# A GNN layer and a mixture of experts on one core: some preparation of the tables done by GpSimd in place of VectorE

## What is computed

```python
def gnn(h, rel, w_ih, w_hh, b_ih, b_hh, src, dst, etype):
    msg = h[src] + rel[etype]
    red = segment_sum(msg, dst, num_segments=6250)
    return gru_cell(red, h, w_ih, w_hh, b_ih, b_hh)

x = x + gnn(layernorm(x), rel, ..., src, dst, edge_type_16)
x = x + experts(layernorm(x))     # top 2 of 8 by x @ Wg + bg; gelu(x @ W1 + b1) @ W2 + b2
```

## Time and profile before

| | |
|---|---|
| median of 3 runs | 1611.08 us (1608.55 to 1616.82) |
| the profiled execution | 1608.13 us |
| its span in the profile | 1606.3 us |
| busy: PE, DVE, ACT, POOL | 83%, 69%, 44%, 64% of the span |
| first gather | 72.29 us |
| last gather | 1195.6 us |

### The profile page before, as it was taken

How to read it: one execution, slowest core, us unless ns; L and a number is a source line. 1 busy time by engine, 2 the same in 40 slices (tenths; PEclk the granted TensorE clock), 3 DMA queues, 4 the chain that set the end, 5 groups by cost and what they waited for, 6 DMA issues and landing times. The chain is left out here.

```text
span 1606.3 us, 37371 instructions
## 1 busy us (share of the span) xinstructions
PE 1333.8 (83%) x12905; PEld 1025.3 (64%) x12905; DVE 1100.4 (69%) x3994; ACT 708.4 (44%) x1538; POOL 1034.2 (64%) x948
## 2 busy tenths in 40 slices
PE   1269999999989999989889998784653899999991
PEld 1235656666656666666667766564653799999991
DVE  7867677577777777778979888953545455555550
ACT  6334444444445554434433332221221676667660
POOL 2177777566777777676777777777773255555552
PEclk9959999999999999999998999686766899999996
DMA  9676544344554455444544544446652455555556
GB/s 304 175 214 197 153 127 114 109 132 133 138 146 137 132 148 143 123 115 142 145 132 146 146 133 112 113 120 211 236 119 60 100 101 94 95 94 96 94 80 179
DMA packets 136158, 220.43 MB, mean 137 GB/s; under 512 B 27761, under 2 KB 101046, under 8 KB 134688
## 3 DMA queue, kind: packets, MB, share of 16 engines
q0 software_dynamic: 63872, 123.12, 31.7%
q1 hardware_dynamic: 72096, 94.84, 19.7%
HBM read 169.05 MB, written 57.76 MB: 141 GB/s over the span
## 5 line engine op out<-in xcount | busy, mean ns | idle before, releaser
L667 POOL DMA_INDIRECT ring<-h_table,idx x728 | 727.2, 999 | 316.2 <-issue 254.8
L780 ACT ACTIVATE amat<-P 128x300 f16<-128x300 f32 (+3 forms) x608 | 230.6, 427 | 398.0 <-PE P L1642 396.2
L1655 PE MATMUL P<-hs,amat 128*126 128x512 f16 (+4 forms) x1323 | 356.9, 399 | 0.0
L721 POOL DMA_INDIRECT out_rows<-yo,xrows x112 | 176.5, 1576 | 162.4 <-DVE yo L1527 114.6
L1140 DVE TENSOR_SCALAR cone<-iota,comb 128x294 f16<-128x294 f16 (+3 forms) x840 | 258.2, 310 | 0.0
L1139 DVE TENSOR_SCALAR lone<-iota,slo 128x128 f16<-128x128 f16 x840 | 223.7, 267 | 15.7 <-PE P L1637 15.2
L1637 PE MATMUL P<-cone,lone 128*128 128x294 f16 (+3 forms) x840 | 164.6, 291 | 52.3 <-ACT amat L780 32.5
L1655 PEld LDWEIGHTS P<-hs,amat 128*126 128x126 f16 (+4 forms) x1323 | 160.7, 137 | 71.9 <-issue 8.2
L1518 DVE SCALAR_TENSOR_TENSOR gl<-gT,scales,gh 128x512 f16<-128x512 f32 x112 | 84.2, 752 | 126.1 <-ACT gh L904 126.1
L1869 PE MATMUL P<-xh,w_all 128*128 128x256 f16 x896 | 157.0, 274 | 0.0
L676 POOL DMA_INDIRECT expert_rows<-xrow,slots x100 | 121.6, 1216 | 54.3 <-issue 26.8
(11 more groups left out here) (240 smaller groups left out, 2666.3 us busy)
## 6 DMA issues: line engine op xcount, KB each, us to landing
raw<-in_L_ffn_W_dram SPq DMA_DIRECT2D x32, 512.0 KB
xrows<-expert_rows SPq DMA_DIRECT2D x56, 257.0 KB, 3.2
ring<-h_table,idx POOLq DMA_INDIRECT x728
w_parts<-parts SPq DMA_DIRECT2D x16, 512.0 KB
w_all<-w_parts SPq DMA_DIRECT2D x8, 1024.0 KB
h_in<-h_table SPq DMA_DIRECT2D x25, 250.0 KB
x<-in_x_dram SPq DMA_DIRECT2D x25, 250.0 KB
out_rows<-x SPq DMA_DIRECT2D x25, 250.0 KB
```

The source lines that it names most:

```text
L667: nc.gpsimd.indirect_dma_start(out=ring[:, r, j, :], out_offset=None, in_=h_dram, in_offset=bass.IndirectOffsetOnAxis(ap=idx[:, slot, g * ...
L721: nc.gpsimd.indirect_dma_start(out=out_dram, out_offset=bass.IndirectOffsetOnAxis(ap=xrows[:, b % XR, j, D:D + 1].bitcast(I32), axis=0), i ...
L780: nc.scalar.activation(amat[:, b % 2, :, s * aw:(s + 1) * aw], P[2 + g % 2][:, 0:HIS * aw].rearrange("p (h w) -> p h w", w=aw), ACT.Copy). ...
L1655: nc.tensor.matmul(both, amat[:, b % 2, hi, 0:used], hs[:, hi, :], start=(hi == 0), stop=False)
```

## The change

Five groups of instructions go from DVE to POOL, in the preamble:
- rest(0), rest(2) and rest(4), with a semaphore `s_rest2`; SP's waits take the one or the other by chunk;
- the splitting of the relation vectors;
- of the source keys the cast of the low bits and the subtraction, which is now float32 on both sides (a cast of the sources first). DVE keeps the mask, ahead of `bases`, and `s_keys` hands it to POOL; `small_weights` waits for POOL's keys.

```diff
+POOL_RESTS = (0, 2, 4)
...
             for c in range(LN_CH + 1):
-                sp.wait_ge(s_rest1, c + 1)
+                if c in POOL_RESTS:
+                    sp.wait_ge(s_rest2, POOL_RESTS.index(c) + 1)
+                else:
+                    sp.wait_ge(s_rest1, c + 1 - sum(n < c for n in POOL_RESTS))
...
 # POOL, behind its two casts, ahead of its waits for s_tr, s_bias and the table
+            def rest(c):
+                pool.wait_ge(s_part1, c + 1)
+                at = hs[:, c * LN_J:c * LN_J + LN_J, :]
+                nc.gpsimd.tensor_tensor(at[:, :, D:PD], xc[:, c % XB, :, :], at[:, :, 0:D], ALU.subtract).then_inc(s_rest2, 1)
+
+            rest(0)
+            rest(2)
+            pool.wait_ge(s_rel, 16)
+            pool_link(nc.gpsimd.tensor_scalar(rel_rest, rel_raw, UP, None, ALU.mult))
+            for part in range(PARTS):
+                pool_link(nc.gpsimd.tensor_copy(rels[:, part, :], rel_rest))
+                if part + 1 < PARTS:
+                    pool_link(nc.gpsimd.tensor_tensor(rel_rest, rel_rest, rels[:, part, :], ALU.subtract))
+            rest(4)
+            pool.wait_ge(s_keys, 1)
+            nc.gpsimd.tensor_copy(slo[:, :], slo_i[:, :])
+            pool_link(nc.gpsimd.tensor_copy(comb[:, :], src_t[:, 0:HEAD * GC]))
+            nc.gpsimd.tensor_tensor(comb[:, :], comb[:, :], slo[:, :], ALU.subtract).then_inc(s_keys, 1)
...
 # DVE, small_weights: the six instructions on the relation vectors go
-                dve.wait_ge(s_rel, 16)
...
+                dve.wait_ge(s_keys, 2)
...
-            rest(0)
             edge_windows()
             rest(1)
             coefficients(3)
             statistics(4)
-            rest(2)
             coefficients(4)
...
             coefficients(6)
-            rest(4)
             rest(5)
             rest(6)
+            dve.wait_ge(s_tr_out, RT)
+            nc.vector.tensor_scalar(slo_i[:, :], src_t[:, 0:HEAD * GC], 127, None, ALU.bitwise_and).then_inc(s_keys, 1)
             bases()
...
 # DVE, head_keys
-                link(nc.vector.tensor_scalar(slo_i[:, :], src_t[:, 0:n], 127, None, ALU.bitwise_and))
-                nc.vector.tensor_copy(slo[:, :], slo_i[:, :])
-                link(nc.vector.tensor_tensor(comb[:, :], src_t[:, 0:n], slo_i[:, :], ALU.subtract))
```

More of the change, by code:

```diff
@@ L451, in gnn_ffn_kernel @@
         names = """
-            s_const s_ones s_pads s_wnat s_weights s_rel s_ln_var s_ln_std s_ln_coef s_ln_h s_part1 s_rest1 s_natf
+            s_const s_ones s_pads s_wnat s_weights s_rel s_ln_var s_ln_std s_ln_coef s_ln_h s_part1 s_rest1 s_rest2 s_keys s_natf
             s_viol s_violb s_natd s_base s_based s_tr s_dst_out s_tr_out s_flag s_bias s_zero s_small s_init
@@ L463, in gnn_ffn_kernel @@
             tx_done xh_ready xl_ready w1_ready l1_done gelu_done g_high g_low l2_done y_out firsts_ready
-            out_written dve_chain late_chain
+            out_written dve_chain late_chain pool_chain
         """.split()
-        (s_const, s_ones, s_pads, s_wnat, s_weights, s_rel, s_ln_var, s_ln_std, s_ln_coef, s_ln_h, s_part1, s_rest1, s_natf,
+        (s_const, s_ones, s_pads, s_wnat, s_weights, s_rel, s_ln_var, s_ln_std, s_ln_coef, s_ln_h, s_part1, s_rest1, s_rest2, s_keys, s_natf,
          s_viol, s_violb, s_natd, s_base, s_based, s_tr, s_dst_out, s_tr_out, s_flag, s_bias, s_zero, s_small, s_init,
@@ L477, in gnn_ffn_kernel @@
          tx_done, xh_ready, xl_ready, w1_ready, l1_done, gelu_done, g_high, g_low, l2_done, y_out, firsts_ready,
-         out_written, dve_chain, late_chain) = [sem(n) for n in names]
+         out_written, dve_chain, late_chain, pool_chain) = [sem(n) for n in names]
         s_nat = [sem(f"s_nat{n}") for n in range(3)]
@@ L659, in _, with pool_link @@
                 nc.gpsimd.tensor_copy(nat[:, c + 1, :, :], nat_i[:, c + 1, :, :]).then_inc(s_natf, 1)
+            made = [0]
+            def pool_link(ins):
+                made[0] += 1
+                ins.then_inc(pool_chain, 1)
+                pool.wait_ge(pool_chain, made[0])
+            def rest(c):
[15 more added lines that the diff above has]
+            nc.gpsimd.tensor_tensor(comb[:, :], comb[:, :], slo[:, :], ALU.subtract).then_inc(s_keys, 1)
             pool.wait_ge(s_tr, 3 * RT + 6)
@@ L1100, in head_keys @@
             def head_keys():
-                n = HEAD * GC
-                link(nc.vector.tensor_scalar(slo_i[:, :], src_t[:, 0:n], 127, None, ALU.bitwise_and))
-                nc.vector.tensor_copy(slo[:, :], slo_i[:, :])
-                link(nc.vector.tensor_tensor(comb[:, :], src_t[:, 0:n], slo_i[:, :], ALU.subtract))
                 for first, end, k, aw, size, c in zone_batches():
```

## The result

| | before | after |
|---|---|---|
| median | 1612.32 us (20 runs) | 1618.66 us (20 runs) |
| ratio | | 1.0039, 95% interval 1.0027 to 1.0050 |
| span of the profiled execution | 1606.3 us | 1614.0 us |
| its mean granted clock | 0.909 | 0.899 |
| first gather | 72.29 us | 80.45 us |

The change makes the kernel slower, by 4.4 to 8.1 us (0.0027 and 0.0050 times 1612.32). That is under the 0.5% that the prediction took for the least that can be told from nothing, but with 20 runs each the interval lies clear of 1; the median is 0.66 us from the forecast of 1618. One of the 20 executions of the kernel before took 1812.12 us; without it the median is 1612.28. Measured again beside ten more runs, the changed kernel stood at 1620.31 against 1611.65, ratio 1.0052 (1.0033 to 1.0071).

The account below looks back on a forecast made before the run. The loop was taken to hang on the first gather, which waits through PE's transposes for DVE's L1005; 5.6 + 3.5 = 9.1 us on 1608.1 gave 1617.2, forecast 1618 with the median's distance, range 1609 to 1625.

Parts of the forecast that it names:

- The bound: Loop start: until about 108 us the loop hangs on the first gather; a gather D us late makes the end D late.
- saved behind the flag: DVE's relation vectors and keys before the loop, 2.1 and 2.0 us: costed at nothing, covered by PE's waits for gathers.
- Step 1: Layer norm: rest(0) on POOL holds DVE's L940, so ACT's normalization of chunk 2 starts at 28.0, +2.7 us.
- The size of POOL's subtraction: Each rest moved to POOL: taken as 3.8 us, bounds 1.9 and 5.7; no profile row showed one.
- Step 2: Layer norm: rest(2) and relation instructions on POOL lose nothing; `std` of chunk 5 at 46.9, still +2.5 us.
- Step 3: Layer norm: rest(4) on POOL holds DVE's L972, +3.8 us; ACT's high part of chunk 5 ends at 59.65, +5.9.
- Step 4: After rest(5), rest(6) and the mask, `bases` starts at 62.7, +5.6 us in all.
- The rival in which only instructions with one input are held: Preamble: only kinds like L940 held, holding by the keys shrinks, rest(4) starts at 48.7; +5.4 us, 1613.5, chance 0.25.
- Step 5: In `bases`: POOL's three key instructions, 0.8 + 0.8 + 1.6 us with waits, hold DVE's small ones; +3.5 us.
- From L1005 to the first gather: End of preamble: L1005 ends near 72.5, the first gather starts near 81.4 (72.29 before).
- From there to the time: Main loop: the first gather's delay carries to the end one to one, 1608.1 + 9.1 = 1617.2 us.
- the 1 us that I added for the distance between median and profiled execution: Whole time: a third of the 3 us by which the median stands above the profiled execution, giving 1618.

Follow-up runs that it names:

- the run with late gathers alone: Kernel before, with POOL's first gather also waiting for DVE's last group number (L1106): 1621.76 us against 1611.65, ratio 1.0068.
- The two runs with the keys behind `bases`: Changed kernel with all rests back on DVE and POOL's keys waiting for DVE's L1005: ratios 1.0011 and 1.0008 against the kernel before.
- the run with added reads: Kernel before plus three 128 x 2048 subtractions on POOL that feed nothing: ratio 1.0046, first gather 82.25 us.
- the second run of the rests: Changed kernel with relation vectors and keys back on DVE, only three rests on POOL, measured again on another chip: ratio 1.0053 against the kernel before.
- the run with the keys alone: Changed kernel with all rests back on DVE, relation vectors and keys still on POOL: ratio 1.0049 against the kernel before.
- The last version: Against the kernel before: only rest(2) and relation vectors on POOL, DVE reordered, two weight blocks before targets, first gathers freed from the others: 1612.26 us, ratio 1.0007; again 0.9984.
- the run with memsets: Kernel before plus two 128 x 3430 float16 memsets on POOL beside `bases`: one run, 1614.36 us.

## Why the prediction was right

**The bound** was read rightly. Both of PE's waits for gathers are in the changed trace, the loop's start moved by 7.73 us where the first gather moved by 8.16, and the run with late gathers alone points the same way. DVE starts the loop 4.7 us later (85.34 for 80.63) while L1005 ends 8.7 us later, so 4.0 us were in fact saved behind the flag, forecast 4.1, and PE's first two waits took up 3.7 of them (1.43 to 4.19, and 1.32 to 2.29). The two runs with the keys behind `bases` show it once more.

**Step 1**: 27.99, forecast 28.0. The size of POOL's subtraction, the term without a row, was 4.05 us for my 3.8; the Trainium skill's 4.5 ("GPSIMD Engine Reference", 3.1 Elementwise) was further off. The 0.25 more cost nothing in step 1: I had allowed 0.6 us for the coefficients behind it, and they took 0.34 (27.62 to 27.96).

**Step 2**: nothing lost, and `std` of chunk 5 at 46.72 (46.9).

**Step 3**: L1002 held to 53.89 (53.3), `std` of chunk 6 at 57.90 (57.8), ACT's high part of chunk 5 to an end of 59.90 (59.65; with the 1.99 us from that `std` to this end in the earlier trace rows the prediction's own 57.8 gives 59.8).

**Step 4**: `bases` from 62.84 (62.7), +5.72 for +5.6. The rival in which only instructions with one input are held forecast rest(4) at 48.7 and most of steps 1 and 3 alike; it is out by L1011, L1012 and L1014, by L957 of the run with added reads, and by the 3.95 us behind rest(0) in the second run of the rests.

**Step 5** was the term that was too large: +3.5 forecast, 8.68 - 5.72 = **+3.0** measured, and 2.8 in the run with the keys alone. POOL's three took 0.88, 0.89 and 1.95 us, more than my 0.8, 0.8 and 1.6, but what counts is the excess of the held ones, 0.85 + 0.80 + 1.82 less 0.17 each, 2.96; L1010 and L1013 ran between the holds, a time that I had counted as lost.

**From L1005 to the first gather** I took the distance of before. PE's weight transposes took 2.83 us for 3.35 before, so 8.68 became 8.16. In the second trace of the changed kernel they took 3.87, and its first gather is at 81.42, the forecast's 81.4. The granted clock in these stretches was 1.00 for the 3.35, 0.98 for the 2.83 and 0.71 for the 3.87: it goes with the longest of the three and leaves the other two unexplained. No step of the change touches these transposes.

**From there to the time** I went one to one, since "nothing in the loop refers to the clock on the wall". Upward this held in the medians, within what they tell: +8.16 and, the second time, +9.13 at the first gather gave +6.3 and +8.7, and +8.79 with late gathers alone gave +10.1. Inside single executions the shift does not stay as it starts. DVE's line L1208 of the earlier trace rows runs once for each of the 25 tiles. In the changed kernel it comes 7.6 us later than before for tile 1, 9.8 for tile 7, 5.2 for tile 17 and 7.4 for the last; with late gathers alone 7.2 for tile 1 and 4.0 for the last. So the agreement of 8.16 with a span of +7.7 is luck in part. It is luck, too, that the forecast is 0.66 us off: the sum was 1.4 us too large for the span, and the 1 us that I added for the distance between median and profiled execution was 1.8 too small (1618.66 less 1615.82 is 2.8).

**What stays open.** Downward, one to one is not shown. The last version's profiled execution is 2.5 us shorter in span, and its head start comes and goes. It is 4.8 us at the first gather, PE's wait at 107.90 is gone, and PE's first matmul on `hs` starts at 106.27 in place of 111.15. But at tile 2 (of the kernel before first, then of this version) nearly nothing is left of it:

```profile
265.94 0.68 DVE L1208 TENSOR_TENSOR oT<-h_h,rT 128x500 f32<-128x500 f32 x1 [1.83 <-ACT rT L819]
265.86 0.68 DVE L1233 TENSOR_TENSOR oT<-h_h,rT 128x500 f32<-128x500 f32 x1 [1.86 <-ACT rT L850]
```

At the last tile it is 3.5. Of the loss 2.5 us fall between 205 and 218 us (ACT's `cts` at 207.16 and 204.57, then at 218.22 and 218.14), where PE's granted clock is lower than before. The windows from 210 to 220 us, again the kernel before first:

```profile
210.00:220.00 10.00, 9.00 (x122) 5.80 (x122) 9.45 (x43) 5.71 (x14) 6.38 (x7) 1.00 0.36 107
210.00:220.00 10.00, 9.33 (x78) 5.20 (x79) 8.23 (x39) 4.65 (x12) 6.92 (x8) 0.73 0.48 130
```

The second trace of the changed kernel loses 3.9 us over the same step, with 0.60 between 220 and 230 us. These are means over windows in which the clock stood in part at the lower of its two levels (1.2 GHz, 2.4 being 1.00). In the 10 us ahead of the window above PE was busy for 7.6 us, and in the kernel before for 8.0, where the clock did not fall. So when the clock falls moves the loop by as much as the shifts that are compared here. Why it falls there in some executions and not in others, and whether this is what takes the head start out of the median, is not shown. Also open is why the rests alone cost more in the whole than at the first gather on the slower chips.

## What to carry to other kernels

Before work is moved from VectorE to GpSimd, list what VectorE runs at that time: in these runs a GpSimd instruction that reads SBUF stopped the next VectorE instruction with two SBUF inputs, or the next tensor_scalar, until it ended, however small that instruction was; a memset stopped a tensor_scalar and a cast, but none with two inputs. Moved work belongs where VectorE runs reductions or statistics, reads PSUM, or waits, and long GpSimd instructions don't belong beside chains of tiny ones. And ask first which event the long stage hangs on: work taken from an engine behind that event (here 4.0 us) only lengthens someone's wait.

## What the runs showed of the hardware

- The holding goes both ways and by the whole instruction: DVE's 0.17 us became 4.07, POOL's 0.66 became 2.59. DVE's statistics ran beside POOL's rest(2) at their usual 2.71 and 0.64 us, and a reciprocal beside the second added subtraction at 0.20. A reduction over 128 x 2048 took its usual 2.29 us beside POOL's casts and subtraction on the relation vectors, which were not stretched either (0.39 and 0.66); no row has one beside a rest.
- Two float32 inputs cost POOL less (3.81 us, measured once) than a float32 and a float16 (4.05), though the second reads fewer bytes. Their tiles also lie differently in SBUF, so the type is not shown to be the cause.
- Casts that read PSUM were not held by POOL's reads (0.69 us beside the keys). L1007 of the run with memsets, a tensor_scalar that reads PSUM, lasted 1.12 us behind the held cast in front of it; whether it was held itself the row doesn't tell.
- The same program takes 1611 us on one chip and 2004 to 2006 on two others. The version with one rest, traced on two of them, has a granted clock of 0.96 and 0.85 between 125 and 600 us, while its preamble up to PE's transposes of the targets differs by 0.6 us.
- The granted clock of one stretch of the loop differs between executions on the same chip: 1.00, 0.73 and 0.60 in three traces around 210 to 230 us, with 2.5 and 3.9 us lost in that step by the latter two.
